# A graph network and expert layers on one core: one bias addition split over a loop, and a table of waits in 16-bit numbers

## The reference, cut to what matters

```python
x = x + _L0_gnn_ref(_layernorm(x, axis=-1), src, dst, edge_weight, ...)
x = x + _L0_ffn_ref(_layernorm(x, axis=-1)[None], ...)[0]
x = x + _L1_gnn_ref(_layernorm(x, axis=-1), edge_index, ...)
x = x + _L1_ffn_ref(_layernorm(x, axis=-1)[None], ...)[0]
```

## Time and profile before

| what | value |
|---|---|
| time, median of three runs | 1832.31 us |
| lowest and highest of the three | 1824.69 and 1832.35 us |
| the profiled execution's own time | 1830.5 us |
| its span in the trace | 1828.7 us |
| PE busy | 1697.4 us, 93% of the span |
| DVE busy | 947.3 us, 52% |
| ACT busy | 569.2 us, 31% |
| the build (about 45 to 548 us) | 503 us |
| the expert block between the second and third message pass (about 1205 to 1340 us) | 135 us |

### The profile page before, as it was taken

How to read it: one execution, slowest core, us unless ns; L and a number is a source line. 1 busy time by engine, 2 the same in 40 slices (tenths; PEclk the granted TensorE clock), 3 DMA queues, 4 the chain that set the end, 5 groups by cost and what they waited for, 6 DMA issues and landing times.

```text
span 1828.7 us, 31285 instructions
## 1 busy us (share of the span) xinstructions
PE 1697.4 (93%) x10117; PEld 1359.1 (74%) x10118; DVE 947.3 (52%) x1613; ACT 569.2 (31%) x854; POOL 187.4 (10%) x263
## 2 busy tenths in 40 slices
PE   6998989888879999999999999999999999998995
PEld 4888888887876777777777777766677777777784
DVE  7999999998973301111044444644322243245436
ACT  2134667788890000000011111234400000004442
POOL 4000000000001100000000000000000000153683
PEclk9999999999999999999999999989999999999998
DMA  4103334454459544445533434900055434534375
GB/s 98 1 29 129 133 157 188 193 213 205 199 239 351 168 146 141 143 146 157 153 117 113 130 116 127 235 35 1 0 185 182 129 110 123 156 116 131 106 240 185
DMA packets 136921, 261.74 MB, mean 143 GB/s; under 512 B 22237, under 2 KB 74736, under 8 KB 136607
## 3 DMA queue, kind: packets, MB, share of 16 engines
q1 hardware_dynamic: 116824, 237.02, 40.0%
q0 software_dynamic: 5808, 14.70, 2.2%
q10 hardware_dynamic: 14230, 9.29, 1.7%
HBM read 161.13 MB, written 108.09 MB: 147 GB/s over the span
## 4 chain that ended last, share of the span: by engine, by line
issue 57%; PE 29%; ACT 6%; DVE 3%; DMA 1%; POOL 1%; ACTq 1%; DVEq 1%; SPq 0%; POOLq 0%
PE ps L2131 12%; PE ps L2162 6%; ACT wide L875 4%; PE ps L2132 4%; PE ps L2383 2%; PE ps L2367 2%; ACT ps L823 1%; PE ps L2375 1%; PE ps L2359 1%; PE ps L2179 0%; DVE act_c L1382 0%; PE ps L2034 0%; PE ps L2191 0%; ACTq L823 0%; DMA wide<-weight_matrix 0%
## 5 line engine op out<-in xcount | busy, mean ns | idle before, releaser
L2162 PE MATMUL ps<-wide 128*128 128x320 f32 (+1 forms) x2000 | 534.9, 428 | 0.0
L2162 PEld LDWEIGHTS ps<-wide 128*128 128x128 f32 x2000 | 379.2, 190 | 142.1 <-issue 1.3
L2131 PE MATMUL ps<-early,act_c 128*128 128x200 bf16 x2400 | 295.6, 252 | 51.5 <-ACT ps L823 30.2
L2131 PEld LDWEIGHTS ps<-early,act_c 128*128 128x128 bf16 x2400 | 220.8, 97 | 65.7 <-issue 65.0
L2162 PE MATMUL ps<-wide,act_a 128*128 128x320 f32 (+1 forms) x1000 | 265.9, 428 | 2.3 <-DMA wide<-weight_matrix 2.3
L2162 PEld LDWEIGHTS ps<-wide,act_a 128*128 128x128 f32 x1000 | 190.7, 191 | 75.9 <-DMA wide<-weight_matrix 2.5
L875 ACT COPY wide<-ps 128x832 f32<-128x832 f32 x200 | 169.9, 850 | 132.7 <-PE ps L2132 130.0
L823 ACT ACTIVATE ps<-wide 128x832 f32 (+1 forms) x200 | 173.4, 868 | 40.9 <-ACT wide L875 32.6
L1382 DVE TENSOR_TENSOR act_c<-act_a,pair_tab 128x3072 bf16<-128x3072 bf16 x98 | 170.4, 1751 | 22.2 <-PE ps L2132 21.7
L1510 DVE TENSOR_TENSOR wide<-ps,rows 128x1280 f32<-128x1280 f32 x10 | 14.9, 1490 | 285.1 <-PE ps L2179 285.1
L2131 PE MATMUL ps<-act_a,act_c 128*128 128x200 bf16 x1152 | 140.2, 251 | 13.5 <-issue 8.5
(11 more groups left out here) (264 smaller groups left out, 1796.1 us busy)
## 6 DMA issues: line engine op xcount, KB each, us to landing
wide<-weight_matrix SPq DMA_DIRECT2D x90, 800.0 KB, 4.5
wide<-count_matrix SPq DMA_DIRECT2D x45, 800.0 KB, 4.5
weight_matrix<-wide SPq DMA_DIRECT2D x60, 480.0 KB, 2.5
count_matrix<-wide SPq DMA_DIRECT2D x60, 480.0 KB, 2.6
weight_matrix<-wide SPq DMA_DIRECT2D x20, 560.0 KB, 2.7
count_matrix<-wide SPq DMA_DIRECT2D x20, 560.0 KB, 2.7
wide<-weight_matrix SPq DMA_DIRECT2D x20, 400.0 KB, 3.7
routed_tokens<-in_x_dram SPq DMA_DIRECT2D x2, 3072.0 KB, 31.0
```

What stands on the lines that cost most here:

```text
L2131: nc.tensor.matmul(weights, hot_parts[:, slot % PART_SLOTS, part, two, :, k], hot_key[mask_slot][:, mask_two, 0:WCOLS, k], start=False, st ...
L2162: i = nc.tensor.matmul(ps[:, 2 * sub + h, 0:n], features[:, q * QUADS + t, h * P:(h + 1) * P], moving, start=q == 0 and t == 0, stop=q == ...
```

## The change

It has two parts. First, the last block's gated bias is added one expert at a time: experts 0, 1 and 2 in the turns of the loop for blocks 1, 2 and 3, ahead of their `ffn_residual`, and expert 3 behind the loop, ahead of `ffn_residual(4)`. There are as many DVE instructions as before, in the same order of experts; in the loop the expert's number is a register.

Second, the tables that PE and ACT load their waits (and PE its bank offsets) from are written as unsigned 16-bit numbers. The working copy stays in 32-bit integers in `early`; the last operation on each part writes the 16-bit table, PE's into the tensor `rows`, ACT's still into `early`. The shift by 9 has become a multiplication by 512. Both bitwise ands with `COUNTED` are gone; on PE a statement of the value's bounds stands in their place, with its run-time check left out. The number of registers loaded is the same.

```diff
-COUNTED = 2047
...
+        line_tab = rows_flat[0:1, at:at + line_cols // 2].bitcast(U16)
...
-        end_tab = early[0:1, line_cols:line_cols + (BUNITS + 1) * ENDS].bitcast(I32)
+        end_tab = early[0:1, line_cols:line_cols + (BUNITS + 1) * ENDS // 2].bitcast(U16)
...
-                    act.wait_ge(pair_done, act.scalar_reg_alu(ALU.bitwise_and, end, COUNTED))
+                    act.wait_ge(pair_done, end)
...
-            dve.tensor_single_scalar(bank_tab, bank_tab, 9, op=ALU.logical_shift_left).then_inc(dve_chain, 1)
+            dve.tensor_scalar_mul(bank_tab, bank_i, 512.0).then_inc(dve_chain, 1)
...
-            dve.tensor_scalar_add(free_tab, free_tab, 1.0).then_inc(dve_chain, 1)
+            dve.tensor_scalar_add(free_tab, free_i, 1.0).then_inc(dve_chain, 1)
...
+            def gated_bias_of(s, e):
+                for t in range(SUPER):
+                    mine = x_nodes[:, ds(s * SUPER + t, 1), :].rearrange("p a f -> p (a f)")
+                    gate = ffn_gate[:, ds(s * SUPER + t, 1), ds(e, 1)].rearrange("p a e -> p (a e)")
+                    bias = expert_bias[:, ds(e, 1), :].rearrange("p e f -> p (e f)")
+                    dve.scalar_tensor_tensor(mine, bias, gate, mine, ALU.mult, ALU.add)
+                dve.drain()
...
             ffn_residual(0)
-            gated_bias(SUPERS - 1)
             with dve.Fori(1, SUPERS - 1) as s:
                 enter(s - 1, 10)
                 apply_gates(s)
                 next_gates(s)
+                gated_bias_of(SUPERS - 1, s - 1)
                 ffn_residual(s)
             leave(SUPERS - 2)
             apply_gates(SUPERS - 1)
+            gated_bias_of(SUPERS - 1, EXPERTS - 1)
             ffn_residual(SUPERS - 1)
...
-                            pe.wait_ge(acc_free, pe.scalar_reg_alu(ALU.bitwise_and, free, COUNTED))
+                            pe.wait_ge(acc_free, nc.s_assert_within(free, 1, WINDOWS // GROUP, skip_runtime_bounds_check_because="a group's number plus one"))
```

More of the change, by code:

```diff
@@ L20 @@
 U32 = mybir.dt.uint32
+U16 = mybir.dt.uint16
 AX = mybir.AxisListType.X
@@ L360, in build_program @@
         rows_flat = rows[:, :, :].rearrange("p a b -> p (a b)")
+        line_cols = PPAD // LINE * LINE_COLS
         key_wide = rows_flat[:, 0:WCOLS].bitcast(BF16).rearrange("p (c k) -> p c k", k=2)
@@ L369, in build_program @@
         pair_dst = rows_flat[:, at:at + PPAD // 2].bitcast(BF16)
+        at += PPAD // 2
+        line_tab = rows_flat[0:1, at:at + line_cols // 2].bitcast(U16)
+        assert at + line_cols // 2 <= 9 * D
+        bank_tab, free_tab = (line_tab.rearrange("p (a q) -> p a q", q=LINE_COLS)[:, :, q] for q in (slice(0, LINE), slice(LINE, LINE_COLS)))
         reached = [early[:, j * PPAD // 2:(j + 1) * PPAD // 2].bitcast(BF16) for j in range(WGROUPS)]
@@ L373, in build_program @@
         window_of, chunk_of = work[:, 1000:1000 + PPAD], degree_row[:, 0:PPAD]
[L375 to L378, removed]
-        end_tab = early[0:1, line_cols:line_cols + (BUNITS + 1) * ENDS].bitcast(I32)
+        line_rows = early[0:1, 0:line_cols].bitcast(I32).rearrange("p (a q) -> p a q", q=LINE_COLS)
+        bank_i, free_i = line_rows[:, :, 0:LINE], line_rows[:, :, LINE:LINE_COLS]
+        end_tab = early[0:1, line_cols:line_cols + (BUNITS + 1) * ENDS // 2].bitcast(U16)
         end_rows = end_tab.rearrange("p (u e) -> p u e", u=BUNITS + 1)[:, :, 0:UGROUPS]
@@ L1306, in _ @@
             dve.wait_ge(windows_taken, 1)
-            dve.tensor_copy(bank_tab, window_of[0:1, :].rearrange("p (a q) -> p a q", q=LINE)).then_inc(dve_chain, 1)
-            dve.tensor_copy(free_tab, window_of[0:1, :].rearrange("p (a b q) -> p a b q", q=QUAD, b=LINE_QUADS)[:, :, :, QUAD - 1]).then_inc(dve_chain, 1)
+            dve.tensor_copy(bank_i, window_of[0:1, :].rearrange("p (a q) -> p a q", q=LINE)).then_inc(dve_chain, 1)
+            dve.tensor_copy(free_i, window_of[0:1, :].rearrange("p (a b q) -> p a b q", q=QUAD, b=LINE_QUADS)[:, :, :, QUAD - 1]).then_inc(dve_chain, 1)
             dve.wait_ge(dve_chain, count(2))
-            dve.tensor_single_scalar(bank_tab, bank_tab, ACCS - 1, op=ALU.bitwise_and).then_inc(dve_chain, 1)
+            dve.tensor_single_scalar(bank_i, bank_i, ACCS - 1, op=ALU.bitwise_and).then_inc(dve_chain, 1)
             dve.wait_ge(next_min, 1)
             dve.tensor_tensor(unsorted, chunk_max, next_ps, ALU.is_gt).then_inc(chunk_ends, 1)
-            dve.tensor_single_scalar(free_tab, free_tab, 1, op=ALU.logical_shift_right).then_inc(dve_chain, 1)
+            dve.tensor_single_scalar(free_i, free_i, 1, op=ALU.logical_shift_right).then_inc(dve_chain, 1)
             dve.wait_ge(dve_chain, count(2))
-            dve.tensor_single_scalar(bank_tab, bank_tab, 9, op=ALU.logical_shift_left).then_inc(dve_chain, 1)
+            dve.tensor_scalar_mul(bank_tab, bank_i, 512.0).then_inc(dve_chain, 1)
             dve.wait_ge(gathered, 3)
             dve.scalar_tensor_tensor(pair_dst, window_of, -32.0 * WIN, over_banks(0), ALU.mult, ALU.add).then_inc(gathered_taken, 1)
-            dve.tensor_scalar_add(free_tab, free_tab, 1.0).then_inc(dve_chain, 1)
+            dve.tensor_scalar_add(free_tab, free_i, 1.0).then_inc(dve_chain, 1)
             dve.wait_ge(pair_windows, 2)
@@ L1715, in second_layer @@
                 dve.sem_inc(side_operand[1], 1)
+            def gated_bias_of(s, e):
[5 more added lines that the diff above has]
+                dve.drain()
             def gated_bias(s):
                 for e in range(EXPERTS):
[L1719 to L1723, removed]
+                    gated_bias_of(s, e)
             with dve.Fori(0, SUPERS - 1) as s:
```

## The result

The changed kernel takes 2230.81 us (median of 4 runs, 2230.25 to 2231.26) against 1831.99 us before (median of 4): ratio 1.2188, 95% interval 1.2158 to 1.2219. The forecast was 1819 us and its range ended at 1836. The change makes the kernel 22% slower, 399 us.

A forecast was written before the change was run, and what follows sets the result against it. PE, busy in 93% of the span, bounds the kernel, so its gaps cost time. Terms -6.3 - 6.8 - 0.4 + 0.25 = -13.2 us gave 1817.3 from the profiled 1830.5, 1819 as a median; range 1797 to 1836.

The forecast's parts named there:

- The register loads: PE's load of 20 numbers per line in the build: one access per number, 64 ns each, so no change from 16 bits.
- The ends of the range: Bounds on PE's load: 716 ns if priced by the byte, or 0.48 us more beside transfers.
- the 16-bit load is dearer: Rival, chance 0.12: line 2116, 74 times, a two-byte number read as a word and cut out; at most 1855 us.
- the same effect in the expert block: Block 1: behind its 3.47 us wait PE ran at 1.2 GHz for a while, granted clock 0.89 against 1.00.
- The gated bias, -6.3 us: Expert block: with the bias away, block 1 takes block 2's 25.56 us instead of 31.87; spread-out instructions cost nothing.
- The ands on PE: Build: a line's first and costs 0.1 us, the other three nothing; removal gains 6.8 us over 68 lines.
- The rival of a queue deep enough to hide the load: Build: TensorE's queue of 64 hides load and and, so only the expert block gains, 1826 us; given little within 0.18.
- DVE's pace as the cap of the build: Build: DVE needs 6.34 us a line, capping it at 469 us, used in the 0.18 rival of byte-priced loads.
- ACT's loads: ACT in the build: only its removed ands were counted, a gain of 0.4 us in the last four groups.
- The tables: At the start on DVE: the operation replacing the shift of line 1315 loses 0.25 us, between 0 and 0.6.
- the confirmation list: What the profile after would show, such as block 1 in 25.6 us and load end to first matmul 0.24 us.

The follow-up runs named there:

- shift: The kernel before with the gated bias in four steps and the 32-bit table of waits moved by one word: 2267.59 us, ratio 1.2188.
- and2: The kernel before with one more bitwise register instruction ahead of each of a line's four waits on PE: 1882.43 us, ratio 1.0116.
- quad8: The kernel before with the gated bias in four steps and two waits for `acc_free` a line instead of four, load unchanged: 1853.23 us, ratio 0.9962.

## Why the prediction was wrong, point by point

- **The register loads: the step that failed.** "By two sizes of the same engine, least values: (1357 - 332) / 16 = 64 ns for each further number of 4 bytes ... 64 ns for four bytes is so long that I take it to be one access per number: no change." Both sizes, 4 and 20, were whole groups of four at a multiple of 16 bytes. The slope was 255 ns for one access of four numbers, not 64 for each. The ends of the range, a byte price and +0.48 us a load, were both of the wrong kind; the true difference was 4718 - 1357 = 3.36 us. A row of the kernel before would have warned of it: the load of five numbers on ACT, in its group of line 864, where the least value is its first load:

```profile
L864 ACTq TENSOR_LOAD <-early x21: 590/1567/1849, 52.0 to 545.7; - x21
```

  A fifth number cost 590 - 332 = 258 ns, four times the supposed 64.
- The rival "the 16-bit load is dearer" had the place and the sign right, its mechanism half (no cutting of words, but lost grouping; `shift` has whole words and the same cost) and its size off by nearly eight: 3.8 us in the middle of the loads against the 0.48 at which it was bounded.
- The Trainium skill's rule, "Runtime: NRT & Kernel Launch", "Instruction fetch mechanics", about 200 ns for each register even in bulk, was set aside because 20 numbers took 1.36 us. Measured is 233 ns for each number that is read alone, near the page's figure, and 64 per number for aligned groups of four, which it does not have.
- **How the 405 us of the build are made up.** The median load is 5596 - 1834 = 3.76 us longer: 74 x 3.76 = 278 us. If the ands that are gone give back what and2's four cost, 21.6 us, that makes an estimated 256 us of gap, where +263 are seen. The rest, 142 us, is PE's busy time at 0.78 of its clock. This part I had not foreseen at all, though I used the same effect in the expert block for 2.8 of the 6.3 us.
- **The gated bias, -6.3 us: right.** Measured -6.1 (3 to 9), block 1 in 25.57 us at a clock of 1.00 with no wait on its broadcasts. The five instructions lie where they were put, 2.07 us before a wait that DVE has anyway; the timeline of DVE:

```profile
1650.15 2.07 DVE L1725 SCALAR_TENSOR_TENSOR x_nodes<-degree_row,ffn_gate,x_nodes 128x256 f32<-128x256 f32 x5
...
1659.12 1.49 DVE L1769 TENSOR_TENSOR wide<-ps,x_nodes 128x1280 f32<-128x1280 f32 x1 [6.90 <-PE ps L2310]
```

- **The ands on PE: the price right, the count wrong.** "The three inside a line come while the sequencer is ahead of PE and cost nothing." Load end to first matmul did fall from 0.34 to 0.25 us, and one more instruction there cost 0.31%, 5.8 us, near the 6.8 of the forecast (its interval reaches from 2 to 10). But the three inside cost 1.12%, 20.8 us, when added. Being ahead was not spare time: it was the stock from which the next load was paid. The rival of a queue deep enough to hide the load fell on the same point: what the sequencer had gained within a line was some 15 pairs, 30 instructions, and a deeper queue would have held no more. "Advanced Engine Details and Errata" of the Trainium skill, section "Engine Queue Depths", gives TensorE a queue of 64.
- **DVE's pace as the cap of the build: right** for its first half. quad8's 6.38 us a line there stands against the 6.34 of the forecast, with DVE waiting for PE for 0.9 us in 240. The 7.20 us a line of the second half are far from it.
- **ACT's loads: wrong**, +12 us for -0.4, the same step as PE's: only the ands were counted there.
- **The tables: nothing** for +0.25 us. The multiplication with 16-bit output takes the 0.77 us of the shift.
- In the confirmation list, "Line 2116 at least 1357 ns again. I'm wrong if that least value has moved by 0.1 us or more" is what found it: 4718 ns, in one row.

## What to carry to other kernels

Price a register load by accesses, not by numbers or bytes: lay the table out in 32-bit words, every load at a multiple of 16 bytes and a multiple of four words long, padded if need be (twelve took 851 ns, ten 1095), and measure before narrowing its type. A slope from two sizes says nothing of sizes, alignments and types that lie outside their common pattern; look for a third row that breaks it. And where a sequencer refills the engine's queue, add up its own time for a whole period, loads included, and compare that sum with the engine's: if it is the larger, each instruction that is added to the loop costs its full slot, ahead of the wait or not. One taken away gives back only what the next limit leaves.

## What the hardware showed that I had not expected

- 32-bit numbers are loaded four at a time if the load begins at a multiple of 16 bytes: 255 ns for four, against 233 ns for each one of 16 bits, and 4.73 to 4.75 us for twenty 32-bit numbers from another start.
- An instruction of the sequencer that is shown as 32 to 46 ns occupies 0.10 to 0.12 us.
- A gap of 3.4 us in a full stream costs PE its clock behind the gap: groups of three matmuls took 0.70 us instead of 0.43 for about 3 us. Splitting the same loads in two (PE's gaps then 1.9 us in the mean) brought the build's clock from 0.78 to 0.89.
- While PE was slow there and until the end of that line, from 165.1 to 168.8 us, the sequencer kept exactly 16 pairs of weight load and matmul ahead of it (counted from the starts of its address instructions and of the weight loads), and its instructions came at PE's pace. So 16 pairs, 32 instructions, were the most that it got ahead in this case, half of the 64 above.
- A register load's length goes with the DMA traffic beside it. In the kernel before the loads of twenty numbers took 1357 to 1378 ns from 52.5 to 125 us, with a DMA share of 0.00, and 2.01 us in the mean from the 39th to the 59th line, with a share of nearly half. No run tests whether the traffic is the cause.
